# A graph decoder's attention turned from float32 matmuls into three float32r passes

## The reference

```python
sig = sigmoid(f1[:, :, None] + f2[:, None, :])            # per head, n x n
att = masked_softmax(adj * sig, adj != 0)                 # both patterns are adj, so att is this alone
Xa  = einsum('hij,hjd->hid', att, Xw)                     # encoder's attention
emb = mlp_block(batchnorm(Xa), enc_mlp ...)               # first dense block
Y   = einsum('hij,hjd->hid', att, emb per head)
Y   = elu(einsum('hnd,hed->hne', Y, W))                   # decoder's attention
out = mlp_block(Y, dec_mlp ...)                           # second dense block
# mlp_block(x): h = elu(x @ Wm.T + bm) + x; batchnorm(h) over the nodes
```

## Time and profile before

| | |
|---|---|
| runs | 3699.71, 3706.84, 3708.70 us; median 3706.84 us |
| the profiled execution | 3702.97 us, its span 3701.1 us |
| PE busy | 3251.3 us, 88% of the span |
| DVE busy | 2320.1 us, 63% |
| ACT busy | 1633.0 us, 44% |
| POOL busy | 238.1 us, 6% |
| moved by DMA | 557.02 MB, mean 151 GB/s |

### The profile page before, as it was taken

How to read it: one execution, slowest core, us unless ns; L and a number is a source line. 1 busy time by engine, 2 the same in 40 slices (tenths; PEclk the granted TensorE clock), 3 DMA queues, 4 the chain that set the end, 5 groups by cost and what they waited for, 6 DMA issues and landing times. The chain is left out here.

```text
span 3701.1 us, 38125 instructions
## 1 busy us (share of the span) xinstructions
PE 3251.3 (88%) x13231; PEld 2093.6 (57%) x13231; DVE 2320.1 (63%) x3048; ACT 1633.0 (44%) x1399; POOL 238.1 (6%) x397
## 2 busy tenths in 40 slices
PE   5799999999977899995999995999999966999995
PEld 4533333333322677773454444777777835888884
DVE  5589888988865466655666554777777744122226
ACT  0288888888832111112222215787777602000002
POOL 0000000000001011110000001000000000000003
PEclk9999999999999899997999997999999988999997
DMA  7500000000013465652222216666566631876654
GB/s 278 196 16 8 16 8 15 15 8 14 7 62 106 168 250 224 240 218 109 97 96 96 96 63 243 240 239 258 225 259 233 240 105 69 356 275 262 265 221 125
DMA packets 109980, 557.02 MB, mean 151 GB/s; under 512 B 12576, under 2 KB 20995, under 8 KB 86064
## 3 DMA queue, kind: packets, MB, share of 16 engines
q1 hardware_dynamic: 90800, 431.91, 30.8%
q0 software_dynamic: 19072, 123.65, 9.2%
HBM read 363.33 MB, written 192.18 MB: 150 GB/s over the span
## 5 line engine op out<-in xcount | busy, mean ns | idle before, releaser
L518 PE MATMUL bank<-dist,hf 128*65 128x512 f32 (+2 forms) x2112 | 830.4, 546 | 64.2 <-ACT dist L480 64.2
L518 PEld LDWEIGHTS bank<-dist,hf 128*65 128x65 f32 x2112 | 277.1, 138 | 609.6 <-issue 457.1
L1345 PE MATMUL bank<-pt,HA 128*128 128x256 f32 x1936 | 504.3, 380 | 3.0 <-DMA HA<-features 3.0
L480 ACT ACTIVATE dist<-dist 128x1408 f32<-128x1408 f32 (+1 forms) x352 | 453.8, 1324 | 1.4
L985 PE MATMUL bank<-HB,pt 128*128 128x512 f32 x968 | 438.4, 594 | 0.0
L1534 PE MATMUL bank<-w,EM 128*128 128x256 f32 x1936 | 426.1, 380 | 12.2 <-DMA w<-weights 12.2
L1534 PEld LDWEIGHTS bank<-w,EM 128*128 128x128 f32 x1936 | 369.0, 191 | 62.9 <-DMA w<-weights 12.4
L1333 PE MATMUL bank<-idt,v 128*128 128x128 f32 x1936 | 304.3, 278 | 78.3 <-ACT pt L1223 50.7
L411 DVE TENSOR_TENSOR dist<-msk,sB 128x1408 f32<-128x1408 uint8 (+1 forms) x208 | 325.6, 1565 | 74.1 <-PE bank L518 65.4
L471 ACT ACTIVATE dist<-dist,neg_t 128x1408 f32<-128x1408 f32 (+1 forms) x208 | 296.3, 1424 | 145.1 <-DVE dist L411 145.1
L1345 PEld LDWEIGHTS bank<-pt,HA 128*128 128x128 f32 x1936 | 328.2, 191 | 26.7 <-DMA HA<-features 3.4
(11 more groups left out here) (153 smaller groups left out, 3707.6 us busy)
## 6 DMA issues: line engine op xcount, KB each, us to landing
w<-weights SPq DMA_DIRECT2D x44, 2816.0 KB, 9.8
weights<-pt SPq DMA_DIRECT2D x220, 512.0 KB, 3.6
al<-in_adj_cols SPq DMA_DIRECT2D x22, 1408.0 KB, 8.2
at<-in_adj_tiles SPq DMA_DIRECT2D x22, 1408.0 KB, 8.2
rows<-in_adj_rows SPq DMA_DIRECT2D x22, 1408.0 KB, 6.8
mrow<-in_adj_rows POOLq DMA_DIRECT2D x22, 1354.0 KB, 6.9
rows_low<-mrow POOLq DMA_DIRECT2D x22, 1354.0 KB, 6.0
rows<-rows_low POOLq DMA_DIRECT2D x22, 1354.0 KB, 8.5
```

The lines of the kernel that those rows point to most:

```text
L480: act.activation(d[:, 0:VALID[c]], d[:, 0:VALID[c]], ACT.Exp, scale=-1.0).then_inc(p_ready, 1)
L518: mm = pe.matmul(sums_bank(hh, k)[0:FW, 0:hi - a * P], hf[hh][:, m, :], d[:, a * P:hi], start=(m == 0), stop=(m == T - 1))
L1345: t = pe.matmul(acc_t[n % 2][:, 0:P2], HA[:, m, h * D3:(h + 1) * D3], pt[n % 2][:, m, :, :].rearrange("p r n -> p (r n)"), start=(m == 0), ...
```

## The change

1. `pair_loop` writes its iterations out instead of a hardware loop.
2. Encoder's attention: of each four units ACT makes the sigmoids in the order 0, 3, 1, 2; the copies `keep(b+1)` to `keep(b+3)` stand at other places; DVE's `weigh` comes after another group.
3. The product with W is split: ACT rounds each tile to float32r (`eh`), DVE takes the rest (`el` = value - `eh`), and both are stored to DRAM (`em_hi`, `em_lo`) for all 22 tiles.
4. Decoder: the head is the outer loop, the chunk of two pairs (512 columns, the last chunk 256) the inner one, n = 0 to 23. The weights come in four pieces of 6, 6, 5 and 5 tiles for both pairs. ACT rounds a piece to float32r (`whi`), DVE subtracts it from the piece in place (`w`), and TensorE does three float32r matmuls per tile: eh*whi, eh*w, el*whi. Features of one head (`eh`, `el`) are loaded from DRAM when the head before is half through.
5. The results of all heads go into `H2`; the second dense block runs only during and after the last head, one chunk behind, and its result overwrites `H2`.

```diff
-BN_RECORDS = [KT * PAIRS, KT * (PAIRS + 6), KT * (2 * PAIRS + 6)]
+SCORE_ORDER = (0, 3, 1, 2)
+WEIGH_AT = (1, 4, 3, 3)
+BN_RECORDS = [KT * PAIRS, KT * (PAIRS + 6), KT * (PAIRS + 12)]
...
 def pair_loop(eng, body, first=0, last=False):
-    lo, hi = int(first), PAIRS - int(last)
-    for i in range(lo):
+    for i in range(PAIRS):
         body(i)
-    with eng.Fori(lo, hi) as i:
-        body(i)
-    if last:
-        body(PAIRS - 1)
...
-                    for u in range(4):
-                        score(u)
+                    for k in SCORE_ORDER:
+                        score(k)
                     for b in range(0, UNITS, 4):
                         more = b + 4 < UNITS
                         expo(b)
-                        if b > 0:
-                            keep(b - 1)
                         expo(b + 1)
                         expo(b + 2)
                         keep(b)
                         expo(b + 3)
                         if more:
-                            score(b + 4)
+                            score(b + SCORE_ORDER[0] + 4)
+                            score(b + SCORE_ORDER[1] + 4)
                         keep(b + 1)
                         if more:
-                            score(b + 5)
+                            score(b + SCORE_ORDER[2] + 4)
                         if b % 8 == 0 and b > 0:
                             ri_out(b // 8 - 1)
-                        if more:
-                            score(b + 6)
                         keep(b + 2)
                         if more:
-                            score(b + 7)
-                    keep(UNITS - 1)
+                            score(b + SCORE_ORDER[3] + 4)
+                        keep(b + 3)
...
-                            if g == 4 and u + 3 < UNITS:
+                            if g == WEIGH_AT[u % 4] and u + 3 < UNITS:
                                 weigh(u + 3)
...
-                            if t % 2:
-                                act.wait_ge(em_mm, t + 1)
-                                act.activation(EM[:, t, :], bank[t % 8][:, :], ACT.Copy).then_inc(em_act, 1)
+                            act.wait_ge(em_mm, t + 1)
+                            if t >= 4:
+                                act.wait_ge(em_stored[t % 4], 32 * (t // 4))
+                            act.activation(eh[t % 4][:, :], bank[t % 8][:, :], ACT.Copy).then_inc(em_act, 1)
...
+                            dve.wait_ge(em_act, t + 1)
+                            if t >= 4:
+                                dve.wait_ge(em_stored[t % 4], 32 * (t // 4))
+                            dve.tensor_tensor(el[t % 4][:, :], bank[t % 8][:, :], eh[t % 4][:, :].bitcast(FP32), ALU.subtract)\
+                                .then_inc(em_dve, 1)
...
+            PIECES = [(0, 6), (6, 12), (12, 17), (17, T)]
+            WS, HS = 5, 3
+            w = [sb(ph, f"w{k}", [P, 2, 6, P2], F32R) for k in range(WS)]
+            whi = [sb(ph, f"whi{k}", [P, 2, 6, P2], F32R) for k in range(HS)]
...
                 @block.sync
+                    for n in range(H3 * NCH):
+                        h, c, width = of(n)
+                        for x, (a, b) in enumerate(PIECES):
+                            k = NPC * n + x
+                            if k >= WS:
+                                sp.wait_ge(piece_done, k - WS + 1)
+                            for r in range(SPANS[c][1]):
+                                sp.dma_start(w[k % WS][:, r, 0:b - a, :].bitcast(FP32),
+                                             weights[H3 * (2 * c + r) + h][:, a:b, :]).then_inc(w_in[k % WS], 16)
+                            if n == 0 and x == 0:
+                                features(0)
...
+                        if c == 3 and h + 1 < H3:
+                            features(h + 1)
...
                 @block.tensor
+                        for m in range(a, b):
+                            hi, lo = whi[k % HS][:, 0:pairs, m - a, :], w[k % WS][:, 0:pairs, m - a, :]
+                            pe.matmul(into, eh[h % 2][:, m, :], hi, start=(m == 0), stop=False)
+                            pe.matmul(into, eh[h % 2][:, m, :], lo, start=False, stop=False)
+                            t = pe.matmul(into, el[h % 2][:, m, :], hi, start=False, stop=(m == T - 1))
+                        t.then_inc(piece_done, 1)
...
+                    for n in range(H3 * NCH):
+                        for x in range(NPC):
+                            attend(n, x)
+                        if n > NCH * (H3 - 1):
+                            mul(n % NCH - 1)
+                    mul(NCH - 1)
...
                 @block.scalar
+                    def split(k):
+                        act.wait_ge(*loaded(k))
+                        if k >= HS:
+                            act.wait_ge(piece_done, k - HS + 1)
+                        pairs, depth = piece(k)
+                        act.activation(whi[k % HS][:, 0:pairs, 0:depth, :], w[k % WS][:, 0:pairs, 0:depth, :].bitcast(FP32),
+                                       ACT.Copy).then_inc(whi_ready, 1)
...
+                    for n in range(H3 * NCH):
+                        c = n - NCH * (H3 - 1) - 2
+                        split(NPC * n)
+                        split(NPC * n + 1)
+                        if n > 0:
+                            first_exp(act, n - 1)
+                        if c >= 0:
+                            second(c, 0)
+                            second(c, 1)
+                        split(NPC * n + 2)
+                        if c >= 0:
+                            second(c, 2)
+                            second(c, 3)
+                        split(NPC * n + 3)
...
                 @block.vector
+                    def rest(k):
+                        dve.wait_ge(whi_ready, k + 1)
+                        pairs, depth = piece(k)
+                        part = w[k % WS][:, 0:pairs, 0:depth, :]
+                        dve.tensor_tensor(part, part.bitcast(FP32), whi[k % HS][:, 0:pairs, 0:depth, :].bitcast(FP32),
+                                          ALU.subtract).then_inc(wlo_ready, 1)
...
                         dve.wait_ge(s_ready, n + 1)
+                        dve.wait_ge(z_done, KT * (c + 1))
+                        dve.scalar_tensor_tensor(out=H2[:, f, a:b], in0=z_t[f][:, 0:b - a],
+                                                 scalar=mlp_nb[:, 1, f:f + 1], in1=s2[n % 2][:, 0:b - a],
                                                  op0=ALU.max, op1=ALU.add).then_inc(h_ready, 1)
...
+                    for n in range(H3 * NCH):
+                        c = n - NCH * (H3 - 1) - 2
+                        rest(NPC * n)
+                        rest(NPC * n + 1)
+                        if n > 0:
+                            first(n - 1)
+                        if c >= 0:
+                            second(c, 0)
+                            second(c, 1)
+                        rest(NPC * n + 2)
+                        if n > 0:
+                            first_end(n - 1)
+                        if c >= 0:
+                            second(c, 2)
+                            second(c, 3)
+                        rest(NPC * n + 3)
```

More of the change, by code:

```diff
@@ L1509, in build, with piece @@
+            def piece(k):
+                a, b = PIECES[k % NPC]
+                return SPANS[k // NPC % NCH][1], b - a
             with nc.Block() as block:
@@ L1527, in _ @@
                 def _(pe):
-                    def attend(n):
-                        h, k = n % H3, n % RING
-                        pe.wait_ge(w_in[k], 16 * (n // RING + 1))
-                        if n >= 2:
-                            pe.wait_ge(at_ready, n - 1)
-                        for m in range(T):
-                            t = pe.matmul(acc_t[n % 2][:, 0:P2], EM[:, m, h * D3:(h + 1) * D3], w[k][:, m, :],
-                                          start=(m == 0), stop=(m == T - 1))
-                        t.then_inc(att_done, 1)
@@ L1538, in mul @@
-                    def mul(p, f):
-                        n = KT * p + f
-                        if f == 0:
-                            pe.wait_ge(y_ready, H3 * (p + 1))
-                        if n >= 2:
-                            pe.wait_ge(h_ready, n - 1)
-                        for k in range(KT):
-                            t = pe.matmul(z_t[n % 2][:, 0:P2], dw[:, k, f * 128:(f + 1) * 128], Y[p % 2][:, k, :],
-                                          start=(k == 0), stop=(k == KT - 1))
-                        t.then_inc(z_done, 1)
@@ new lines, in mul @@
+                    def mul(c):
+                        a, b = CHUNKS[c]
+                        pe.wait_ge(y_ready, NCH * (H3 - 1) + c + 1)
+                        if c == 0:
+                            pe.wait_ge(dw_in, 16)
+                        else:
+                            pe.wait_ge(h_ready, KT * c)
+                        for f in range(KT):
+                            for k in range(KT):
```

(41 more changed lines are left out.)

131 lines of the change are left out of this document (70 added, 61 removed).

## The result

The changed kernel takes 3694.07 us (median of 20 executions, 3682.46 to 3706.85), the kernel before 3706.88 us beside it (20 executions, 3698.66 to 3717.4): a ratio of 0.9965, 95% interval 0.9953 to 0.9978, 12.8 us less. The forecast was 3676. Direction and range held; the gain came out at less than half of the 27 to 31 us forecast. The profiled execution took 3685.27 us against 3702.97, 17.7 less, and the traces are compared on these two.

A forecast was written before the change was run, and what follows sets the result against it. TensorE was taken to bound the old decoder (496.8 of 515 us busy) and mostly the encoder's attention. Attention -40, embedding +6, decoder +8 and loops -1 sum to -27 on 3703.0: 3676 us, range 3640 to 3716.

The forecast's parts named there:

- Attention (-40): Encoder's attention: the new order cuts the four-unit block period from 31.63 to 29.7 us, 1.9 in each of 21 blocks.
- Rival B: Encoder's attention gives nothing, its stall growing back to 3: saved 0 to 10 us, 3706 to 3716; chance 0.17.
- Embedding through DRAM and the start (+6, and 20.5): Embedding: extra DVE operations and the last store cost 6 us; decoder start: first loads and pipeline filling take 20.5.
- Decoder on TensorE alone (340): Decoder: float32r matmuls need 340 us of TensorE instead of 416, 76 less; 256-column ones taken at 0.12 us.
- The DVE chain (17.3 a unit): Decoder, heads 0 to 2: DVE's waits and work set 17.3 us per 512-column unit, not TensorE's 15.4; 98.5 a head.
- Start and feature loads: Decoder: start takes 20.5 us; feature loads of heads 1 to 3 stall 4 to 5 each, 13 together (bounds 0, 30).
- about 3 us of slack: Decoder's weight pieces: a load may take 8.6 us and a 1536 KB piece takes some 6.8.
- Rival C: Decoder: pieces arrive late; at 9.6 us a landing, units take 19.2, +40 us, total 3716; chance 0.15.
- Last head (190): Decoder's last head with the second dense block: units of 17.3, 31.1, 3 x 32 and 27.5, plus tail, 190 us.
- Loops (-1): Loops written out in the stages ahead: branches go, work stays, -1 us, bounds -10 and +5.
- Rival E: Written-out loops starve the engines of instructions: over +15 us in four stages, 3692 to 3720; chance 0.05.
- Rival D: Decoder runs at TensorE's pace: 3 x 13.5 us less, 3636, or 3655 with half of it; chance 0.13.

The follow-up runs named there:

- features_rows: The changed kernel with the split embedding stored by head, so a partition's features load in one run of 11,264 bytes: 3685.38 us, 0.9947 of the kernel before.
- early_split_no_reload: The changed kernel with ACT rounding the third piece ahead of the exponential, and no decoder weight loads after the first five pieces: 3637.85 us (one run).
- no_reload: The changed kernel without the decoder's weight loads after the first five pieces, features still loaded: 3656.77 us (one run, before 3703.37).
- combined_spread: The changed kernel with features by head, small chunk in two pieces, early third-piece rounding, reordered last head, features loaded in four parts: 3626.58 us, 0.9784 of before.
- last_head_order: The changed kernel with the third piece's split put ahead of the first two quarters of the dense block's results: 3670.02 us, 0.9883 of the kernel before.

## Why the prediction was right or wrong

**Attention (-40): right in size and cause.** ACT's timeline, one block apart:

```profile
2613.77 2.56 ACT L1213 ACTIVATE v<-v,nm 128x2708 f32<-128x2708 f32 x1
...
2622.35 2.56 ACT L1213 ACTIVATE v<-v,nm 128x2708 f32<-128x2708 f32 x1 [0.37 <-POOL nm L1191]
...
2642.99 2.55 ACT L1213 ACTIVATE v<-v,nm 128x2708 f32<-128x2708 f32 x1
...
2652.59 2.56 ACT L1213 ACTIVATE v<-v,nm 128x2708 f32<-128x2708 f32 x1 [1.39 <-POOL nm L1191]
...
2673.23 2.55 ACT L1213 ACTIVATE v<-v,nm 128x2708 f32<-128x2708 f32 x1
```

The rows without a wait are the first exponentials of three blocks. The period is 29.22 from the first to the second, but 30.24 from the second to the third. From the third period of the stage on, 29.2 and some 29.9 take turns, and its 21 periods add to 622.4 where before they added to 664.9. The mean is 29.64 (forecast 29.7, before 31.66). The wait of 3.40 for `nm` is 0.37 and 1.39 in turn, and in three blocks the weight-load side of the waits for `pt` fell from 9.5 to

```profile
PEld bank L1327 <- ACT pt L1220: 1.8, 3, 1.4
```

once a block in place of twice. 42.5 us are saved in the 21 periods, and the first exponential of the stage comes 2.7 later (23.2 behind its start for 20.5), which the prediction put at nothing: 39.9 together. So the period was right to 0.1 us, and the exact hit is luck only in so far as two small errors, of 2.5 and 2.7, cancel. The runs with this part alone give 17 to 36, less than the trace: 6 of it stood ahead of the attention in its profiled execution, where the lists are those of before. Rival B, which decides from a period of 31.2, is out.

**Embedding through DRAM and the start (+6, and 20.5): right.** 48.0 to the first `at`, forecast 46. The start's load of 2.88 MB of features in 512-byte runs was put at 9.7 us, 28 ns a run; the rate during it is

```profile
3087.00:3095.00 8.00, 0.00 (x0) 0.00 (x0) 3.36 (x1) 2.76 (x1) 0.00 (x0) 0.50 1.17 300
```

300 GB/s, so 9.6 us; from the landing of the first piece (3088.53) to that of `el` (3098.43) it is 9.9. In `features_rows`, with features in runs of 11,264 bytes, the rate of the same stage is

```profile
3096.00:3100.00 4.00, 0.00 (x0) 0.00 (x0) 0.00 (x0) 1.37 (x1) 0.00 (x0) 0.50 1.04 435
```

The Trainium skill's three cycles a packet (DMA: Bandwidth & Descriptors, "Why small descriptors are slow (HBM only)"), by which I had estimated 7.9 us, is too cheap by this row.

**Decoder on TensorE alone (340): right.** float32r matmuls of 512 columns stand 0.227 apart. For those of 256, of which no row stood, the forecast took 0.12, and the timeline of `early_split_no_reload` has just that:

```profile
3195.73 0.28 PE L1579 MATMUL bank<-whi,eh 128*128 128x256 f32 x1
3195.85 0.28 PE L1580 MATMUL bank<-w,eh 128*128 128x256 f32 x1
```

With loads and chain out of the way a head takes 86.9 where the count gave 85: five units of 15.05 and a small one of 11.6, in which TensorE stops once for 2.8 us, while DVE subtracts two full pieces of the next unit.

**The DVE chain (17.3 a unit): right place, a little dear.** A unit takes 16.7, without a load in it too. The rows from `at` at 3158.75 to the subtraction that starts at 3162.36 are the prediction's walk: 3.6 from start to start, forecast 3.7 (3.1 to 6.8). Moving ACT's rounding ahead of the exponential takes it to 15.0, as it should if this is the chain. Without loads a head takes 94 where the walk gave 98.5: five units of 16.7 for 17.3, and 10.4 for the small one's 12. Over TensorE's own pace that is 21.2 in three heads, not the 40.5 put down.

**The step that failed: "Start and feature loads", the 13 us for features and the "about 3 us of slack" of the pieces.** With `no_reload` as the measure the loads cost 37.8 in three heads. Two things were missed. The features' lump costs its whole transfer, 28 in three heads, because no slack of 3 us is there to take a part of it. The slack was the 8.6 us that a load may take, less 6.8 for a piece of 1536 KB, worked out from the 9.8 of the earlier trace rows, loads of a decoder whose DMA engines were 66% busy. Between 3226 and 3261, in ordinary units, the halves of such pieces alone take 7.9 in the median:

```profile
w<-weights SPq DMA_DIRECT2D x8, 768.0 KB, 7.9
```

And whole first pieces of the units at n = 3, 8 and 9 land 8.7, 9.2 and 9.8 us after they are issued. ACT takes each of them within 0.02 us of its landing. And the small unit, priced "by the same walk" of ACT and DVE, had no loads in its price: with four of the ring's five places holding half a piece, the loads fall behind by another 9. Rival C was right that the DMA engines would bind, but not in its form: it priced every unit at 19.2 and the stage 40 dearer, and the ordinary units stayed at 16.7. The stage's bytes should have been divided by a rate at the outset. The DMA rows of the stretch:

```profile
DMA packets 40329, 107.91 MB, mean 338 GB/s; under 512 B 2478, under 2 KB 23471, under 8 KB 40316
...
w<-weights SPq DMA_DIRECT2D x66, 768.0 KB, 7.4
w<-weights SPq DMA_DIRECT2D x66, 640.0 KB, 7.1
eh<-embedded_hi SPq DMA_DIRECT2D x3, 1408.0 KB, 12.9
el<-embedded_lo SPq DMA_DIRECT2D x3, 1408.0 KB, 16.5
```

107.91 MB are 249 us at the 434 of the earlier trace rows and 279 at its 387, against the 295.5 forecast by the chain. The division alone would not have named the loads as the bound; it shows that some 17 us in 296 are all the room they have at the lower rate, and `combined_spread`, with the DMA engines busy 99% of the time, takes 279. The prediction set the landing times of single transfers against a slack and never made that division, though it had both rates.

Part of the 37.8 is not stall but clock: PE's busy time is 269.5 in the changed kernel and 259.3 in `no_reload` for the same matmuls, 10 of the 37.8, with the granted clock at 0.93 instead of

```profile
3134.20:3416.00 281.80, 259.31 (x1189) 208.96 (x1188) 228.30 (x127) 175.22 (x90) 0.00 (x0) 0.99 0.18 47
```

0.99.

**Last head (190): 8 short, and its order avoidable.** Units with `mul` took 31.9, 33.5, 30.9 and 29.0, about as drawn (32 each, 27.5 for the small unit's). From the last `at` to the statistics it is 35.7; by DVE's rows the first result behind `mul(4)` came 13.8 after it, as forecast, and `mul(5)` took 9.6 (from the end of DVE's work ahead of it) instead of 6.9, 2.7 of the 8:

```profile
3600.87 0.75 DVE L1689 SCALAR_TENSOR_TENSOR H<-bank,mlp_nb,s 128x512 f32<-128x512 f32 x1 [8.97 <-PE bank L1594]
...
3618.30 0.48 DVE L1689 SCALAR_TENSOR_TENSOR H<-bank,mlp_nb,s 128x256 f32<-128x256 f32 x1 [5.49 <-PE bank L1594]
...
3622.74 0.85 DVE L1053 BATCH_NORM_AGGREGATE bn_mv<-rec 128x2 f32<-128x36 f32 x4
```

`mul(5)` had been priced at 0.43 us for each of its 16 matmuls. TensorE had stood idle for 7.33 us before it, and the granted clock from 3608 to 3618 is 0.70, where it was 1.00 under `mul(4)` (3587 to 3600). The stall of "about 3.3" behind `second` is the 2.92 of TensorE's row above, its place and size as written. What the prediction did not say is that it is a matter of order: `last_head_order` takes 20 out of this stretch.

**Loops (-1): inside its bounds, with a small gain.** -5.6 by the runs (bounds -10, +5). Rival E is out. Rival D, TensorE's pace, is what `early_split_no_reload` shows to be there once the loads are out; with all loads in, `combined_spread` comes to 279 of its 260.

**Sum.** Forecast -27; measured -17.6 in the traces: loops and executions -10, attention 0, decoder +21 (start +2, heads 0 to 2 +11, last head +8). In the heads +11 is itself a difference of two errors, loads +25 and chain and pace -14 (260.6 + 21.2 = 281.8 against 295.5). The first says what was missed; the second hid half of it.

## What to carry to other kernels

When a stage gets faster on its engine, divide its bytes by the rate that the DMA engines reach in the rows of this kernel, at this length of run, before following any chain: here 108 MB at the 387 GB/s of the earlier trace rows gave 279 us beside 260 of TensorE, and with so little room a lump of other loads, or a ring that shrinks with its pieces, is paid for in full. Count a ring in bytes, not in buffers. Spreading the lump over the phase before was worth 6 of 285 us here, since the bytes bind all the same.

A releaser is only the last link. TensorE waited for DVE in all 18 stalls, and the longest of them began two engines further back, in a load; an experiment that takes the loads out and one that reorders ACT, and both together, part the two.

Work of an outer stage that runs beside the last of an inner loop belongs behind the operations on which the busiest engine waits: the same instructions in another order were worth 20 us.

## What the runs showed of the hardware

- The DMA engines are over 94% busy at very different rates: 300 GB/s with runs of 512 bytes, 385 for the mix of pieces (rows of 5 and 6 KB) with features spread, 435 at 11 KB. The busy share doesn't tell them apart (1.17, 0.99, 1.04). The length of the run alone does not order them either: 2 KB runs had 387.
- SyncE's issue of `el` in 512-byte runs held its list for 8.67 us in the middle of a head (3154.31), and the next piece of `w` was asked for only behind it; in runs of 11 KB the same issue took 1.47.
- Float32r matmuls keep the rate of their columns down to 256: 0.12 us, and 0.227 for 512.
- A short stall of TensorE can cost more than its length. Behind the stall of 2.92 us at 3487.23 the next tiles stand 1.28 us apart (3488.25, 3489.53) where they stood 0.68 (3480.07, 3480.75): four tiles took 4.5 us in place of 2.7, until 3491.69, at the lower of TensorE's two clocks (matmuls of 0.63 us for 0.39). That is 1.7 on top of 2.9. It need not: behind a stall of the same 2.92 at 3554.31, two units later, the tiles stand 0.69 apart at once:

```profile
3554.31 0.50 PE L1580 MATMUL bank<-whi,eh 128*128 128x512 f32 x1 [2.92 <-DVE w L1656]
...
3555.11 0.40 PE L1580 MATMUL bank<-whi,eh 128*128 128x512 f32 x1
...
3555.80 0.39 PE L1580 MATMUL bank<-whi,eh 128*128 128x512 f32 x1
```

Behind the stalls of about 9 us between 11 and 15 matmuls run at the lower clock. What decides it these runs don't show.
